# A block of gated values in its natural row order in DRAM, picked apart by the loads instead of by the store

## The chip, the cores and the metric

The kernel runs on one core of one Trainium2 chip. The metric is the device time of one execution in microseconds (us), lower is better. It is a single launch, and the numbers of this document are medians of several executions, or are read from one execution that the hardware profiler recorded.

## What is computed

The input is 8 sequences of 1024 tokens with 512 float32 channels. Two layers with residuals follow each other. The first is an adapter picked by the sequence's language (512 to 128 to 512), with a layer norm. The second is a recurrent cell, and the change lies in it. Cut to what matters:

```python
x = x + layernorm(x + relu(x @ W1 + b1) @ W2 + b2) * gamma0 + beta0      # per language
ctx    = causal_ema(x, tau_ctx)                     # h[t] = alpha * h[t-1] + x[t]
wg     = sigmoid(concat(x, ctx) @ Wg.T + bg)
gated  = x * wg                                     # "g" in the kernel
mod    = 0.5 + sigmoid(gelu(x @ Wn1.T + bn1) @ Wn2.T + bn2)      # 8 values per token
traces = [causal_ema(gated * mod[:, d], tau[d]) for d in range(8)]
temporal = sum_d traces[d] * softmax(blend)[d]
gate = sigmoid(temporal @ Wtemp.T + btemp)
soma = gelu(x @ Wsoma.T + bsoma)
x = x + layernorm((soma * gate) @ Wout.T) * gamma1 + beta1
```

## The kernel before

The 8192 tokens are worked off in 16 tiles (k = 0 to 15) of 512 tokens, two to a sequence. A tile has NB = 4 blocks of P = 128 tokens, and a block has NI = 4 spans of L = 32 tokens. `slot(k)` is written once for each engine; in slot k an engine does the end of tile k-1, the recurrence of tile k and the first layer of tile k+1, in a fixed order written out by hand. There is no planner: each engine runs its own list in order, and semaphores join the lists.

Large products run as three passes over a value split into a high and a low part (`split_product`, all its matmuls are recorded at L861). PE is TensorE, DVE VectorE, ACT ScalarE, POOL GpSimd. SP (SyncE) issues every DMA and computes nothing; all DMAs share its one queue.

The recurrence of a tile goes so:

- `value_gate(b)` (PE, L861) makes the gate's logits of block b, `gate_logits(b)` (DVE, L768) adds the bias, `open_gate(b)` (ACT, L490) takes the sigmoid, and `gated(b)` (DVE, L772) multiplies with x. The result is `g[:, b, :]` in SBUF, one token per partition, 512 floats (2 KB) each. It is signalled by `g_ready`.
- The recurrence inside the spans needs another arrangement, `grep` (4 spans by 512 channels in each partition): partition q*32 + s holds, for q = 0 to 3, the tokens s, 32+s, 64+s and 96+s of the block. [...] There are two buffers, `grep[b % 2]`.
- `products(b, hh, c)` (DVE, L763, four per block) multiplies `grep` with weights into `U`. `within_spans(b, hh)` (PE, L1005) takes U against the decay tables `Arep`.
- `span_states()` (PE at L987, DVE at L778) gives the states of the spans, V, and needs all four blocks of g. `from_before(b)` (PE, L1014) adds what comes from earlier spans. `trace(b)` (ACT, L494), `trace_by_channels(b)` (PE, L1026), `trace_high(b)` (ACT, L439) and `trace_low(b)` (DVE, L651) turn the result for the next product.

SP's list around the change, for one tile, is: `store_spans(0)`, `repeat_spans(0)`, `store_spans(1)`, `store_spans(2)`, `repeat_spans(1)`, `store_spans(3)`, `repeat_spans(2)`, `repeat_spans(3)`, then the store of x1 of the next tile (`keep_x1`, L277), and in the next slot the loads of x (L269) and of its transpose (L272). In this list `store_spans(b)` waits for `g_ready` of block b. `repeat_spans(b)` waits until the store of block b has landed (`g_stored[b]`, L320), and for b = 2 and 3 also until the products of block b-2 have been made (L322), since the buffer is theirs. For b = 1 there is no second wait.

DVE's list around it is: `gate_logits(2)`, `gated(2)`, products (0,0,0) and (0,0,1), `gate_logits(3)`, product (0,1,0), `gated(3)`, products (0,1,1) and (1,0,0), `span_states`, the last three products of block 1, the first two of block 2, `trace_low(0)`, the other two of block 2, the first two of block 3, `trace_low(1)`, and the last two. PE's is `value_gate(3)`, `soma_of(1)`, `within_spans(0, ...)`, `span_states`, `soma_begun(2)`, `from_before(0)`, `within_spans(1, 0)`, `soma_ended(2)` and so on. So PE can't pass the wait for V at `from_before(0)`, and V stands in DVE's list behind the first product of block 1.

Of the kernel before, what the change touches and what calls it, by code (L numbers as in the profile page):

```python
# [4 lines left out]
P = 128  # L5
BATCHES, SEQ, C = 8, 1024, 512
# [5 lines left out]
NB = TOK // P  # L12
NC = C // P
L = 32
NI = P // L
# [25 lines left out]
def cond_resid_kernel(nc, x, xc, ids, w1, w2, b1, b2, g0, be0, wg, wn1, wsoma, wtemp, wout, wn2,  # L41
                      bg, g1, be1, cols, taus, bn2, blend, eye, bits, out):
    F = mybir.dt.float32
# [8 lines left out]
    with ctx:  # L52
        def sb(name, shape, dt=F):
            return ctx.enter_context(nc.sbuf_tensor(name, shape, dt))

        def sb_two_ways(name, shape):

            with nc.sbuf_tensor(f"{name}_f", shape, F) as plain:
                pass
            return plain, sb(f"{name}_r", shape, R)  # L60
# [4 lines left out]
        def sem(name):  # L65
            return ctx.enter_context(nc.semaphore(name))
# [37 lines left out]
        grep = [sb(f"grep_{n}", [P, NI, C]) for n in range(2)]  # L104
# [11 lines left out]
        g, soma_hi = sb_two_ways("g", [P, NB, C])  # L116
# [9 lines left out]
        mv0, mv1 = (V[0][:, at:at + 2 * NB].rearrange("p (b s) -> p b s", s=2) for at in (192, 208))  # L126
        rows4 = sb("rows4", [P, 4, NB])
        rstd0, rstd1, minus_half, ema_last = (rows4[:, n, :] for n in range(4))
        g_dram = nc.dram_tensor("g_spans", [NB, L, NI * C], F, kind="Internal").ap()
        x1_dram = nc.dram_tensor("x1_tiles", [2, P, NB * C], F, kind="Internal").ap()  # L130


# [31 lines left out]
        g_stored = [sem(f"g_stored{n}") for n in range(NB)]  # L164
        grep_in = [sem(f"grep_in{n}") for n in range(2)]
# [32 lines left out]
        def upto(per_tile, tile, j):  # L198

            return tile * per_tile + (j + 1)  # L200

        def parts_of(k):

            return 0 < k <= TILES, 0 <= k < TILES, 0 <= k + 1 < TILES
# [49 lines left out]
        @block.sync  # L254
        def _(sp):
            def load_language(batch):

                one = sp.value_load(lang[0:1, batch:batch + 1], min_val=0, max_val=LANGS - 1)
                sp.dma_start(W1[:, :, :], w1[bass.ds(one, 1)].rearrange("a (n p) m -> p (a n) m", p=P)).then_inc(ld_lang, 16)
                sp.dma_start(W2_raw[:, :], w2[bass.ds(one, 1)].rearrange("a p m -> p (a m)")).then_inc(ld_lang, 16)  # L260
                sp.dma_start(b1_col, b1[bass.ds(one, 1)].rearrange("a (p m) -> p (a m)", p=P)).then_inc(ld_lang, 16)
                for row, src in ((b2_row, b2), (gamma0_row, g0), (beta0_row, be0)):
                    sp.dma_start(row[:, :], src[bass.ds(one, 1)].to_broadcast([P, C])).then_inc(ld_lang, 16)

            def load_split(n, src):
                sp.dma_start(halves[n][2], src.rearrange("(n p) m -> p n m", p=P)).then_inc(ld_split[n], 16)

            def load_x(tile):
                sp.dma_start(x_t[:, :, :], x[tile].rearrange("(n p) c -> p n c", p=P)).then_inc(ld_x, 16)  # L269

            def load_xT(tile):
                sp.dma_start(xT[:, :, :], xc[tile].rearrange("(n p) t -> p n t", p=P)).then_inc(ld_xT, 16)  # L272

            def keep_x1(tile):

                sp.wait_ge(x1_ready, upto(4, tile, NB - 1))
                sp.dma_start(x1_dram[tile & 1], x1[tile & 1][:, :, :].rearrange("p b c -> p (b c)")).then_inc(x1_stored, 16)  # L277

            def first_loads():

                sp.dma_start(lang[:, :], ids).then_inc(ld_ids, 16)
                sp.dma_start(alpha[:, 0, :], taus).then_inc(ld_small, 16)
                sp.dma_start(blend_c, blend).then_inc(ld_small, 16)
                sp.dma_start(con, bits).then_inc(ld_small, 16)
                sp.dma_start(ident[:, :], eye).then_inc(ld_small, 16)
                sp.dma_start(col, cols).then_inc(ld_small, 16)
                sp.dma_start(bn2_row[:, :], bn2.to_broadcast([P, D])).then_inc(ld_small, 16)
                load_xT(0)
                sp.wait_ge(ld_ids, 16)
                load_language(0)  # L290
                load_x(0)
                load_split(0, wn1)
                load_split(1, wsoma)
                load_split(2, wg[0:C])
                sp.dma_start(Wn2[:, :], wn2).then_inc(ld_rows, 16)
                for row, src in ((bg_row, bg), (gamma1_row, g1), (beta1_row, be1)):
                    sp.dma_start(row[:, :], src.to_broadcast([P, C])).then_inc(ld_rows, 16)

            def second_loads():

                sp.wait_ge(full["h"], upto(1, 0, 0))
                load_xT(1)
                load_split(3, wg[C:2 * C])
                sp.wait_ge(x1_ready, upto(4, 0, NB - 1))
                load_x(1)
                load_split(4, wtemp)
                load_split(5, wout)
                keep_x1(0)

            def slot(k):  # L310
                has_prev, has_cur, has_next = parts_of(k)

                def store_spans(b):
                    sp.wait_ge(g_ready, upto(4, k, b))
                    sp.dma_start(g_dram[b].rearrange("s (i c) -> i s c", i=NI), g[:, b, :]).then_inc(g_stored[b], 16)

                def repeat_spans(b):


                    sp.wait_ge(g_stored[b], 16 * upto(1, k, 0))  # L320
                    if b >= 2:
                        sp.wait_ge(U_ready, upto(PIECES, k, 4 * (b - 2) + 3))  # L322
                    elif b == 0 and has_next:
                        sp.wait_ge(x1_ready, upto(4, k + 1, NB - 1))
                    for q in range(NQ):
                        sp.dma_start(grep[b % 2][q * L:(q + 1) * L, :, :].rearrange("p i c -> p (i c)"),  # L326
                                     g_dram[b]).then_inc(grep_in[b % 2], 16)

                if has_prev:
                    if has_next:  # L330
                        if k & 1:
                            load_language((k + 1) // 2)
                        sp.wait_ge(U_ready, upto(PIECES, k - 1, 3 * PIECES // 4 - 1))
                        load_x(k + 1)
                        sp.wait_ge(U_ready, upto(PIECES, k - 1, PIECES - 1))
                        load_xT(k + 1)
                        sp.wait_ge(full["h"], upto(1, k + 1, 0))
                    else:
                        sp.wait_ge(U_ready, upto(PIECES, k - 1, PIECES - 1))
                    sp.dma_start(x1_back[:, :, :].rearrange("p b c -> p (b c)"), x1_dram[(k - 1) & 1]).then_inc(ld_back, 16)  # L340
                    for b in range(NB):
                        sp.wait_ge(res_ready, upto(4, k - 1, b))
                        sp.dma_start(out_tiles[k - 1, b * P:(b + 1) * P, :], res[:, b, :]).then_inc(stored, 16)
                else:
                    second_loads()
                if has_cur:
                    store_spans(0)
                    repeat_spans(0)
                    store_spans(1)
                    store_spans(2)  # L350
                    repeat_spans(1)
                    store_spans(3)
                    repeat_spans(2)
                    repeat_spans(3)
                if has_next:
                    sp.wait_ge(x1_stored, 16 * upto(1, k, 0))
                    keep_x1(k + 1)

            first_loads()
            for k in range(TILES + 1):  # L360
                slot(k)
            sp.wait_ge(stored, 16 * NB * TILES)
            sp.wait_ge(x1_stored, 16 * TILES)
# [795 lines left out]
```

## Time and profile before

| | us |
|---|---|
| median of 3 runs | 1514.78 |
| lowest, highest | 1514.3, 1514.91 |
| the profiled execution | 1509.55 |
| its span, first to last instruction | 1507.8 |
| PE busy in the span | 1372.3 (91%) |
| DVE busy | 1019.1 (68%) |
| ACT busy | 515.4 (34%) |
| POOL busy | 393.2 (26%) |
| mean granted clock of PE | 0.975 |
| mean DMA rate | 124 GB/s |

How to read it: busy times are sums over the whole span, and "busy" for PE counts modelled ends of pipelined matmuls, so 91% is not PE at its peak. The page's other parts used below are the chain of work that ended last (the last instruction followed back through what released it), the list of DMA issues with the median time from issue to landing, the waits by who waited for whom, timelines of one engine in order of time, and tables by stretch ("windows") with the busy time of each engine, the granted clock of PE as a fraction of full speed, the share of time in which the 16 DMA engines were busy, and what they moved.

### The profile page before, as it was taken

To read this page: it belongs to the slowest core of one execution; us is meant where nothing else is said; L and a number is where in the kernel's file an instruction comes from. 1 tells how busy PE (TensorE), PEld (TensorE's weight loads), DVE (VectorE), ACT (ScalarE), POOL (GpSimd) and SP (SyncE) were. 2 spreads that over 40 slices of the span, in tenths; PEclk is the share of its full clock that TensorE was granted. 3 is DMA by queue.
4 is the path that set the end of the run, shared out by engine and by line. 5 is a ranking of instruction groups with operands and counts; after the bars stand their busy time and mean duration, and the time that the engine had idled before them with its cause. 6 is when DMAs were issued, how large, how long until landed. Compare 5 with 4: busy or idle time off the path is not lost.

```text
span 1507.8 us, 19538 instructions
## 1 busy us (share of the span) xinstructions
PE 1372.3 (91%) x7836; PEld 977.2 (65%) x7836; DVE 1019.1 (68%) x1493; ACT 515.4 (34%) x812; POOL 393.2 (26%) x295
## 2 busy tenths in 40 slices
PE   2689989999999999999998998999999999998985
PEld 1566858576685766757576685757758576685744
DVE  6868676685667857577684767668576685767363
ACT  2324333242333424333242423424233332433323
POOL 4314123041330504123041422304133050411103
PEclk8799999999999999999999999999999999999999
DMA  7354351825427063361715526172541806334150
GB/s 240 112 144 143 95 161 60 203 77 138 141 61 226 35 165 109 107 194 49 201 44 144 170 71 181 57 193 93 134 146 58 228 29 168 113 99 125 49 144 32
DMA packets 66140, 186.22 MB, mean 124 GB/s; under 512 B 9090, under 2 KB 13826, under 8 KB 53762
## 3 DMA queue, kind: packets, MB, share of 16 engines
q1 hardware_dynamic: 66050, 184.97, 42.3%
q8 instruction: 62, 1.02, 0.3%
q14 instruction: 28, 0.23, 0.0%
HBM read 134.61 MB, written 50.33 MB: 123 GB/s over the span
## 4 chain that ended last, share of the span: by engine, by line
DVE 24%; DMA 21%; PE 19%; issue 13%; ACT 12%; SPq 3%; POOL 3%; POOLq 0%; DVEq 0%
DMA g_spans<-g_f 12%; PE ring L861 10%; DMA grep<-g_spans 9%; DVE U L763 7%; PE Tp L1014 4%; PE Tp L1005 4%; SPq L326 3%; ACT U L482 2%; DVE x L701 2%; DVE V L706 2%; DVE U L645 2%; DVE seq_lo L651 2%; DVE soma_r L659 2%; PE ring L854 2%; ACT g_r L448 2%
## 5 line engine op out<-in xcount | busy, mean ns | idle before, releaser
L763 DVE TENSOR_TENSOR U<-grep,w_qs 128x1024 f32<-128x1024 f32 x256 | 301.9, 1219 | 102.8 <-DMA grep<-g_spans 102.6
L385 POOL TENSOR_TENSOR x<-grep,b_row 128x512 f32<-128x512 f32 x64 | 81.9, 1312 | 668.1 <-DMA grep<-in_x 668.1
L1005 PE MATMUL Tp<-U,Arep 128*32 128x256 f32 x2048 | 153.0, 404 | 14.8 <-DVE U L763 13.8
L768 DVE TENSOR_TENSOR g_f<-ring,bg_row 128x512 f32<-128x512 f32 x64 | 44.2, 690 | 156.7 <-PE ring L861 156.6
L394 POOL TENSOR_TENSOR grep<-grep,beta_row 128x512 f32<-128x512 f32 x64 | 93.6, 1494 | 179.9 <-DMA grep<-x_tiles 179.9
L490 ACT ACTIVATE g_f<-g_f 128x512 f32<-128x512 f32 x64 | 40.5, 632 | 254.9 <-DVE g_f L768 254.7
L494 ACT ACTIVATE T_sb_f<-Tp 128x512 f32<-128x512 f32 x64 | 38.2, 598 | 260.7 <-PE Tp L1014 260.7
L1005 PEld LDWEIGHTS Tp<-U,Arep 128*32 128x32 f32 x2048 | 54.0, 112 | 105.0 <-DVE U L763 47.9
L861 PE MATMUL ring<-Wout_hi,g_r 128*128 128x512 f32 x256 | 102.2, 399 | 19.5 <-DVE soma_r L659 19.5
L861 PE MATMUL ring<-seq_hi,Wtemp_hi 128*128 128x512 f32 x256 | 106.8, 417 | 8.5 <-DVE seq_lo L651 8.5
L1014 PE MATMUL Tp<-V,Epow 128*128 128x512 f32 x128 | 76.7, 683 | 41.0 <-DVE V L778 41.0
L861 PE MATMUL ring<-x1T_hi,Wsoma_hi 128*128 128x512 f32 x256 | 109.8, 429 | 0.0
L861 PE MATMUL ring<-Wg_hi,seq_hi 128*128 128x512 f32 x256 | 100.4, 392 | 7.4 <-DVE Wg_r L562 7.4
L861 PE MATMUL ring<-Wg_hi,x1T_hi 128*128 128x512 f32 x256 | 103.1, 403 | 0.0
L861 PE MATMUL ring<-x1T_lo,Wsoma_hi 128*128 128x512 f32 x256 | 102.1, 399 | 0.0
L861 PE MATMUL ring<-x1T_hi,Wsoma_r 128*128 128x512 f32 x256 | 101.4, 396 | 0.0
L861 PE MATMUL ring<-Wout_r,g_r 128*128 128x512 f32 x256 | 100.4, 392 | 0.0
L861 PE MATMUL ring<-Wg_r,seq_hi 128*128 128x512 f32 x256 | 100.3, 392 | 0.0
L861 PE MATMUL ring<-Wout_hi,soma_r 128*128 128x512 f32 x256 | 100.2, 392 | 0.0
L861 PE MATMUL ring<-Wg_hi,seq_lo 128*128 128x512 f32 x256 | 100.1, 391 | 0.0
L861 PE MATMUL ring<-seq_hi,Wtemp_r 128*128 128x512 f32 x256 | 100.0, 391 | 0.0
L861 PE MATMUL ring<-Wg_hi,x1T_lo 128*128 128x512 f32 x256 | 100.0, 390 | 0.0
(151 smaller groups left out, 2865.5 us busy)
## 6 DMA issues: line engine op xcount, KB each, us to landing
grep<-g_spans SPq DMA_DIRECT2D x256, 256.0 KB, 5.0
grep<-in_xc SPq DMA_DIRECT2D x16, 1024.0 KB, 7.2
grep<-in_x SPq DMA_DIRECT2D x16, 1024.0 KB, 9.0
x_tiles<-x SPq DMA_DIRECT2D x16, 1024.0 KB, 7.6
g_spans<-g_f SPq DMA_DIRECT2D x64, 256.0 KB
grep<-x_tiles SPq DMA_DIRECT2D x16, 1024.0 KB, 4.8
out<-U SPq DMA_DIRECT2D x64, 256.0 KB, 2.0
gamma_row<-in_g SPq DMA_DIRECT2D x9, 256.0 KB, 7.3
```

Of the source, the lines that this page charges most:

```text
L326: sp.dma_start(grep[b % 2][q * L:(q + 1) * L, :, :].rearrange("p i c -> p (i c)"), g_dram[b]).then_inc(grep_in[b % 2], 16)
L385: nc.gpsimd.tensor_tensor(new[:, b, :], x_t[:, b, :], b2_row[:, :], ALU.add).then_inc(xb2_ready, 1)
L394: nc.gpsimd.tensor_tensor(x1_back[:, b, :], x1_back[:, b, :], beta1_row[:, :], ALU.add).then_inc(x1b_ready, 1)
L448: nc.scalar.activation(soma_hi[:, e, :], soma[:, e, :], ACT.Identity).then_inc(somahi_ready, 1)
L482: nc.scalar.activation(res[:, b, :], res[:, b, :], ACT.Identity, scale=rstd1[:, b:b + 1]).then_inc(scaled_ready, 1)
L490: nc.scalar.activation(g[:, b, :], g[:, b, :], ACT.Sigmoid).then_inc(sig_ready, 1)
L494: nc.scalar.activation(T_sb[b % 2][:, :], Tp[b % 2][:, :], ACT.Identity).then_inc(T_ready, 1)
L763: V_.tensor_tensor(U[:, (n + 2) % 4, :, :], grep[b % 2][:, :, at], w_qs[:, hh, at].unsqueeze(1).to_broadcast([P, NI, HC]), ALU.mult).then_ ...
L768: V_.tensor_tensor(g[:, b, :], bank_of("wg", k, b)[:, :], bg_row[:, :], ALU.add).then_inc(pre_ready, 1)
L861: last = nc.tensor.matmul(dst, lhsT(a, n), rhs(b, n), start=(first and n == begin and m == 0), stop=(final and n == steps - 1 and m == 2))
L1005: last = nc.tensor.matmul(Tp[b % 2][i * L:(i + 1) * L, at], Arep[:, b * NI + i, hh, :], U[:, (n + 2) % 4, i, :], start=(hh == 0 and c == 0 ...
L1014: nc.tensor.matmul(Tp[b % 2][:, :], Epow[:, odd * NB + b, :], V[odd][:, :], start=False, stop=True).then_inc(full["T"], 1)
```

## The change

The tensor in DRAM changes its shape from 32 rows of 8 KB per block (a row is one s with its four spans side by side) to the block's own 128 rows of 2 KB. Before, the store took the rows of 2 KB to their places in rows of 8 KB, through a destination that is walked as span, s, channel (sizes 4, 32, 512). Now the store writes the block as it stands in SBUF, 128 rows to 128 rows. The loads in turn read for each partition four pieces of 2 KB that lie 64 KB apart, where they read one row of 8 KB. The bytes in `grep`, the number of DMAs, their sizes, all waits and the order of every list are as before.

```diff
-        g_dram = nc.dram_tensor("g_spans", [NB, L, NI * C], F, kind="Internal").ap()
+        g_dram = nc.dram_tensor("g_blocks", [NB, P, C], F, kind="Internal").ap()
@@ store_spans(b)
                     sp.wait_ge(g_ready, upto(4, k, b))
-                    sp.dma_start(g_dram[b].rearrange("s (i c) -> i s c", i=NI), g[:, b, :]).then_inc(g_stored[b], 16)
+                    sp.dma_start(g_dram[b], g[:, b, :]).then_inc(g_stored[b], 16)
@@ repeat_spans(b)
                     for q in range(NQ):
-                        sp.dma_start(grep[b % 2][q * L:(q + 1) * L, :, :].rearrange("p i c -> p (i c)"),
-                                     g_dram[b]).then_inc(grep_in[b % 2], 16)
+                        sp.dma_start(grep[b % 2][q * L:(q + 1) * L, :, :],
+                                     g_dram[b].rearrange("(i s) c -> s i c", i=NI)).then_inc(grep_in[b % 2], 16)
```

## Rows read from the trace of the kernel before

**Rows 1.** The page's chain of work that ended last, by line, shares of span.
```profile
DMA g_spans<-g_f 12%; PE ring L861 10%; DMA grep<-g_spans 9%; DVE U L763 7%; PE Tp L1014 4%; PE Tp L1005 4%; SPq L326 3%; ACT U L482 2%; DVE x L701 2%; DVE V L706 2%; DVE U L645 2%; DVE seq_lo L651 2%; DVE soma_r L659 2%; PE ring L854 2%; ACT g_r L448 2%
```

**Rows 2.** Waits: who waited for whom, us in total, times, longest.
```profile
DVE U L763 <- DMA grep<-g_spans: 102.6, 50, 5.3
...
PE Tp L1014 <- DVE V L778: 41.0, 16, 3.9
```

**Rows 3.** Timeline of SP's issues in tile 7: start, us, line, what.
```profile
710.28 0.59 SPq L315 DMA_DIRECT2D g_spans<-g_f  x1
716.16 1.73 SPq L326 DMA_DIRECT2D grep<-g_spans  x4
717.93 4.45 SPq L315 DMA_DIRECT2D g_spans<-g_f  x2
725.09 1.70 SPq L326 DMA_DIRECT2D grep<-g_spans  x4
727.66 0.51 SPq L315 DMA_DIRECT2D g_spans<-g_f  x1
728.84 10.96 SPq L326 DMA_DIRECT2D grep<-g_spans  x8
```

**Rows 4.** Timeline of DVE in tile 7; in brackets idle before and releaser.
```profile
715.12 0.69 DVE L772 TENSOR_TENSOR g_f<-g_f,x 128x512 f32<-128x512 f32 x1 [0.60 <-ACT g_f L490]
...
721.16 0.69 DVE L772 TENSOR_TENSOR g_f<-g_f,x 128x512 f32<-128x512 f32 x1 [0.70 <-ACT g_f L490]
722.94 2.36 DVE L763 TENSOR_TENSOR U<-grep,w_qs 128x1024 f32<-128x1024 f32 x2 [1.09 <-DMA grep<-g_spans]
725.21 0.68 DVE L768 TENSOR_TENSOR g_f<-ring,bg_row 128x512 f32<-128x512 f32 x1
...
732.30 1.22 DVE L763 TENSOR_TENSOR U<-grep,w_qs 128x1024 f32<-128x1024 f32 x1 [3.54 <-DMA grep<-g_spans]
...
739.05 2.36 DVE L763 TENSOR_TENSOR U<-grep,w_qs 128x1024 f32<-128x1024 f32 x2 [1.52 <-DMA grep<-g_spans]
...
745.38 2.36 DVE L763 TENSOR_TENSOR U<-grep,w_qs 128x1024 f32<-128x1024 f32 x2 [1.10 <-DMA grep<-g_spans]
```

**Rows 5.** Timeline of PE in tile 7, behind its wait for V.
```profile
734.19 1.12 PE L1014 MATMUL Tp<-V,Epow 128*128 128x512 f32 x2 [1.99 <-DVE V L778]
```

**Rows 6.** Page's DMA issues: count, KB each, median us to landing.
```profile
grep<-g_spans SPq DMA_DIRECT2D x256, 256.0 KB, 5.0
...
grep<-in_x SPq DMA_DIRECT2D x16, 1024.0 KB, 9.0
...
grep<-x_tiles SPq DMA_DIRECT2D x16, 1024.0 KB, 4.8
out<-U SPq DMA_DIRECT2D x64, 256.0 KB, 2.0
```

**Rows 7.** Windows: stretch, us, busy by engine, granted clock, DMA share, GB/s.
```profile
712.00:716.00 4.00, 4.00 (x49) 3.09 (x48) 1.67 (x4) 0.63 (x1) 0.00 (x0) 1.00 0.22 63
...
727.00:734.00 7.00, 5.20 (x50) 2.63 (x49) 3.46 (x5) 1.55 (x2) 0.00 (x0) 1.00 1.02 247
...
753.00:755.00 2.00, 2.00 (x19) 1.73 (x16) 1.49 (x3) 2.00 (x5) 2.00 (x2) 1.00 1.02 397
```

**Rows 8.** Timelines of DVE and SP in tile 8, the latest of the tiles.
```profile
809.32 0.69 DVE L772 TENSOR_TENSOR g_f<-g_f,x 128x512 f32<-128x512 f32 x1 [0.70 <-ACT g_f L490]
...
813.73 1.70 SPq L326 DMA_DIRECT2D grep<-g_spans  x4
```

**Rows 9.** Windows: the 4 us behind the wait for V in tile 6.
```profile
643.50:647.50 4.00, 3.43 (x18) 1.10 (x18) 3.92 (x4) 0.60 (x1) 0.00 (x0) 0.57 0.54 129
```

**Rows 10.** Windows from store 0 of a tile to the next's: tiles 1, 2, 6.
```profile
170.05:258.16 88.11, 83.76 (x490) 59.94 (x489) 60.36 (x90) 30.84 (x49) 23.67 (x18) 1.00 0.42 120
258.16:350.31 92.15, 87.11 (x492) 61.57 (x491) 63.55 (x91) 31.81 (x51) 23.98 (x18) 0.96 0.46 129
...
619.87:710.28 90.41, 85.72 (x492) 60.77 (x491) 63.34 (x91) 31.93 (x51) 23.98 (x18) 0.98 0.46 132
```

## The prediction, made blind

> **What bounds the kernel now.** I read the chain of work that ended last first, to see which transfers stand on the path. The store of the gated block holds 12% of the span, the load that reads it back 9%, and issuing those loads 3% [rows 1]. The list of waits gives the same from the consumer's side: DVE stood 102.6 us before its products for the loads, and PE stood 41.0 us in 16 waits, one per tile, for V [rows 2]. PE is busy 91% of the span. So most of a tile is bound by PE, and one stretch by the way of the block through DRAM.
>
> The timelines show that stretch, here in tile 7. SP issues store 0 at 710.28 and the first load of block 0 at 716.16, which it may do once the store has landed: 5.88 us for 256 KB [rows 3]. Block 1 is what counts. Its values are ready at 715.81 (715.12 + 0.69) [rows 4], SP still waits for store 0, then issues four loads, and gets to store 1 at 717.93. Store 1 lands at about 725.05, and the load of block 1 starts at 725.09 [rows 3]. DVE gets it at 732.30, after 3.54 us of idling [rows 4]; PE, which needs V, made just behind that first product, has been idle for 1.99 us at 734.19 [rows 5]. The load of block 2 arrives at 739.05 and that of block 3 at 745.38; DVE waits for both, 1.52 and 1.10 us [rows 4]. So from 725 to 745 three loads follow each other, and the tile ends some 5 us behind the last.
>
> **The store: what it costs now and then.** A store of the same size and the same pieces, 128 rows of 2 KB, is in the kernel already: the output, with a destination that is just 128 rows. It lands 2.0 us after issue (median of 64), where the gated block's takes 5.88 [rows 3, 6]. In the window in which only that store moves, the 16 DMA engines are busy 0.22 of the time, which is three and a half engines, at 63 GB/s [rows 7]. A destination walked with 4 as its outermost size has evidently been dealt to few engines. After the change the outermost size is 128, as for the output, and I take 2.0 us.
>
> The Trainium skill has the rule for it (DMA: Bandwidth & Descriptors, section "Why a DMA increments its semaphore by 16 and not by 1"): a DMA runs on the largest number of engines up to 16 that divides the slowest dimension of both sides. That gives 4 before and 16 after, and the share of 0.22 agrees; by it the sum is the same as mine.
>
> **Where the gain goes, block by block**, in tile 7.
>
> Block 0: the store lands at 712.3, the loads are issued by 714.1 and land 5.0 us after issue [rows 6], about 719. Before they were awaited until 722.94. But in DVE's list the products stand behind `gated(2)`, which ends at 721.85, and behind two products comes `gate_logits(3)` at 725.21, which needs PE's `value_gate(3)` [rows 4]. So 1.09 us of waiting for the load turns into about 1 us of waiting for PE, and block 0 gives nothing.
>
> Block 1: store 1 is issued at 715.85, when it is ready, behind the loads of block 0 in the same queue, and lands with them or about 1 us behind, by 720.5. SP next has store 2 in its list, which waits for `gated(2)`: 721.87. It takes 0.51 us to issue, so the loads of block 1 start at 722.4 in place of 725.09: 2.7 us earlier. Here the wait for the store is replaced by the wait for the third block. In tile 8 the same two rows give 809.32 + 0.69 + 0.55 = 810.6 against 813.73, 3.1 us [rows 8]; the other tiles I read lie between 2.5 and 3.1. From first issue to DVE the load took 7.21 us, and a store spread over all engines now runs half a us ahead of it: 256 KB at the 247 GB/s of a full stretch [rows 7] is 1.1 us, of which at most half falls behind the load's own issue. I take 7.3: arrival at 729.7, against 732.30, so 2.6 us.
>
> PE then isn't kept: V would be ready at 729.7 + 1.2 + 0.6 = 731.5, and PE's work before it ended near 732.2 (734.19 less 1.99) [rows 5]. All of that idling goes.
>
> Block 2: its loads are issued at 728.84 as before, since product (0,1,1) hangs on PE and `gated(3)`. They landed 10.2 us later, because block 1 was on the wire. The gap between arrivals was 6.75 us for 1 MB, which at 247 GB/s needs 4.25; between them lay store 3, with all its bytes on a few engines. It now costs every engine the same 1.1 us. So the arrival lies between 729.7 + 5.4 = 735.1 and 729.7 + 6.75 = 736.4, against 739.05: 2.6 to 3.9 us.
>
> Block 3: issued when block 1's products are made, before at 737.6 (inside the row of 728.84, the last 8 us after its start), now at 729.7 + 1.2 + 0.6 + 3.5 = 735.0. It took 7.75 us, now 6.7 (four issues of 0.43 and 5.0) to 7.75: 741.7 to 742.8 against 745.38, so 2.6 to 3.6 us. Behind it the same products, two `trace_low` and PE's last pieces follow in 5 to 6 us. PE had about 14.4 us of work between 735.2 and 751.2, and starts on it at 733, so it permits up to 3.6 us. I take 2.6 us per tile, and 16 times that is 42 us.
>
> **The clock.** Behind the wait for V, PE's granted clock fell to half (1.2 GHz) in most tiles: over the four us behind it, tile 6 shows 0.57 [rows 9], and of sixteen such windows eleven lie between 0.50 and 0.73, five at 1.00. PE had been idle just before, 2.6 us in the mean and 3.9 at most [rows 2]. With that idling gone I expect no fall there. What a fall costs is bounded by whole tiles: tiles 2 and 6, with the same work, took 92.15 and 90.41 us, the first with a mean clock of 0.96, the second with 0.98 [rows 10]. So between 0 and 1.7 us each; most even tiles are like the cheap one, in which later waits hid the slow stretch. I take 0.9 for eleven tiles, 10 us.
>
> **The loads.** Their rows of 8 KB become four pieces of 2 KB. Nothing in the trace shows just that. From below: with every row 8 KB the loads keep the engines at a share of 1.02 and move 247 GB/s; in a window in which the transposed x is loaded, in pieces of 2 KB that also lie apart, the same share moves 397 GB/s [rows 7]. So a piece of 2 KB costs an engine 0.08 us, and 32 of them 2.6 us, under the 4.25 that a load has in any case; something other than the size of the pieces sets 247, and the price is nothing, or a little below. From above: 1 MB of x in pieces of 2 KB takes 9.0 us to land, 1 MB of x1 in rows of 8 KB 4.8 [rows 6]; all of that difference, 4.2 us, is the dearest it can be. But x is issued behind the last load and the 1 MB store of x1 in the same queue, which explains the 9.0 without the pieces. I take 0, being nearest to the window of 397. SP's issue of a load stays near 0.43 us; if 128 pieces cost it what they cost store 3, 0.51 us [rows 3], a block's four issues would take 0.3 us more, which is inside the range.
>
> The Trainium skill would explain the 247 (SBUF — State Buffer, section "Door 1: The DMA port swizzle"): 32 or 64 neighbouring partitions reach only 8 of 16 ports. By it the pieces are free. Against the change stands its rule of a fixed overhead of about 3 cycles per packet (DMA: Bandwidth & Descriptors, "Why small descriptors are slow (HBM only)"): 4 x 67 cycles for 259, 3.5% of 4.25 us, 0.15 us a load; by that the sum would be some 5 us smaller. No run here shows it.
>
> **The sum.** 42 + 10 = 52 us off the profiled execution's 1509.55 is 1457.5. The median lies 5.2 above that execution, so 1514.78 - 52 = 1463. Nothing else changes: between the tile's end and the next store 0 each engine's list starts from that end, x is loaded earlier by the same amount, and output stores are untouched.
>
> **Rivals.**
>
> Only part is passed on (15%). Store 1 lands late behind the loads, or PE, ACT and the trace steps behind block 3 take half back, as they may with 1.5 us less of slack. 1 to 1.6 us per tile and 5 us of clock: 21 to 31 us, 1484 to 1494. Against it: 1.3 us of room between store 1's landing and its use, and 3.6 us of room on PE.
>
> The loads eat the store's gain (8%): slower than before. Three loads in a row lie on the path, the first and third in full, since block 2's is overlapped. With a price d per load the arrival of block 3 is 742.3 + 2d against 745.38, so it decides from d = 1.5 us, a third of the data's time. With d halfway to the bound, 2.1, it is 1.1 us per tile, 18 us: 1533; at 4.2 about 5.5 us, 1603. For it speaks only the row of 9.0 us.
>
> The change doesn't do what it says (4%): the store isn't spread and keeps its 5.9 us. Then nothing moves, and it is 1512 to 1517. Against it stands the output's row of the same form.
>
> **Chances and range.** The forecast has 73%, its own range 2.0 to 3.4 us per tile and 3 to 14 us of clock: 35 to 68 us, 1447 to 1480. With most of the first rival the range is 1446 to 1490. By 0.2%, about what a measurement of this kernel can tell from no change: faster 0.88, the same 0.05, slower 0.07.
>
> **What would show it.** After the change, the time from store 0's issue to SP's first load issue should be near 2.1 us. The loads of block 1 should start 0.55 us behind the end of `gated(2)`. DVE's waits for the loads should fall from 102.6 to some 30 us, and PE's for V from 41.0 to under 5, with the clock at 1.00 behind it; DVE's wait for PE at L768 should grow by about 16 us. The load's median of 5.0 us tells d: over 6.5 the slower rival holds. If the loads arrive earlier as said and the tile doesn't, the steps behind block 3 are what I misjudged.

## The result, and the profile after

The changed kernel takes 1455.46 us (median of 4, 1450.32 to 1457.57) against 1514.54 us for the kernel before on the same chip: a ratio of 0.9608, 95% interval 0.9581 to 0.9636. That is 59 us less, where 52 were forecast (1463 us, range 1447 to 1480). The profiled execution has a span of 1454.6 us, 53.2 less than before.

The chain that ended last, by engine and by line, on the page of the changed kernel:

```profile
PE 64%; DVE 20%; ACT 5%; issue 3%; DMA 2%; POOL 1%; SPq 0%; POOLq 0%; DVEq 0%
PE ring L861 51%; DVE U L763 6%; PE Tp L1005 5%; DVE soma_r L659 4%; PE Tp L1014 4%; DVE U L645 3%; DVE seq_lo L651 2%; DMA grep<-g_blocks 2%; ACT g_r L448 2%; DVE soma_f L656 2%; DVE x1T_lo L633 2%; PE ring L854 2%; ACT T_sb_f L494 2%; PE smp L968 1%; PE smp L987 1%
```

The store of the block, 12% of the chain in [rows 1], is gone from it, and the load has gone from 9% to 2%. PE's own work, the product helper at L861 above all, now leads to the end. The waits (us in total, times, longest) and the DMA issues (median us to landing last) say the same:

```profile
DVE g_f L768 <- PE ring L861: 179.7, 62, 6.4
...
DVE U L763 <- DMA grep<-g_blocks: 16.5, 29, 1.3
```

```profile
grep<-g_blocks SPq DMA_DIRECT2D x256, 256.0 KB, 4.4
...
g_blocks<-g_f SPq DMA_DIRECT2D x64, 256.0 KB, 2.0
```

DVE waits 16.5 us for the loads in place of 102.6, and PE's wait for V, 41.0 us in [rows 2], is no longer in the list. What grew is DVE's wait for PE at L768. The store lands in 2.0 us, as the output's does in [rows 6]; the load lands in 4.4 where it took 5.0.

Tile 11 is typical of the changed kernel. SP's issues (start, us, what), which answer to [rows 3]; L315 stores a block of gated values to DRAM, L326 reads it back in four loads of 32 partitions each:

```profile
1032.74 0.33 SPq L315 DMA_DIRECT2D g_blocks<-g_f  x1
1034.77 1.75 SPq L326 DMA_DIRECT2D grep<-g_blocks  x4
1038.30 6.38 SPq L315 DMA_DIRECT2D g_blocks<-g_f  x2
1044.72 1.87 SPq L326 DMA_DIRECT2D grep<-g_blocks  x4
1050.12 0.34 SPq L315 DMA_DIRECT2D g_blocks<-g_f  x1
1051.30 7.73 SPq L326 DMA_DIRECT2D grep<-g_blocks  x8
```

And DVE in the same tile, answering to [rows 4]:

```profile
1043.62 0.69 DVE L772 TENSOR_TENSOR g_f<-g_f,x 128x512 f32<-128x512 f32 x1 [0.70 <-ACT g_f L490]
1044.23 2.35 DVE L763 TENSOR_TENSOR U<-grep,w_qs 128x1024 f32<-128x1024 f32 x2
1047.67 0.69 DVE L768 TENSOR_TENSOR g_f<-ring,bg_row 128x512 f32<-128x512 f32 x1 [1.09 <-PE ring L861]
...
1051.49 1.23 DVE L763 TENSOR_TENSOR U<-grep,w_qs 128x1024 f32<-128x1024 f32 x1 [0.26 <-DMA grep<-g_blocks]
1053.14 0.69 DVE L778 TENSOR_TENSOR V<-smp,w_jd 120x512 f32<-120x512 f32 x1 [0.42 <-PE smp L987]
...
1057.83 2.36 DVE L763 TENSOR_TENSOR U<-grep,w_qs 128x1024 f32<-128x1024 f32 x2 [0.60 <-DMA grep<-g_blocks]
...
1067.79 2.35 DVE L763 TENSOR_TENSOR U<-grep,w_qs 128x1024 f32<-128x1024 f32 x2
```

Store 0 has landed at 1034.77, 2.03 us behind its issue (5.88 before). The loads of block 1 are issued at 1044.72, 11.98 us behind store 0, 0.41 us behind the end of `gated(2)` (1043.62 + 0.69); in tile 7 of before it was 14.81. DVE gets block 1 at 18.75 us behind store 0, in tile 7 of before at 22.02. Tile 7 itself went from 22.02 to 19.60, its third block of values being ready 0.8 us later than before; the mean over tiles 1 to 13 went from 22.5 to 19.1. V no longer waits for the load but for PE (0.42 us). The last product ends at 1070.14, 37.40 us behind store 0.

I call that time, from store 0's issue to the end of the last product, the stage, and what is left up to the next store 0 the tail. Read off the timelines in the same way for the 14 tiles 0 to 13:

| us | before | after |
|---|---|---|
| 14 tiles, store 0 to store 0 | 1260.8 | 1213.0 |
| of it stages | 582.1 | 527.1 |
| of it tails | 678.7 | 685.9 |
| one stage, tiles 1, 5, 7, 9, 13 of before (clock stays up) | 40.1 to 40.3 | |
| one stage, tiles 2 to 4, 6, 8, 10 to 12 (clock falls) | 41.3 to 43.4 | |
| stage of tile 0 | 43.8 | 38.2 |
| one stage after, tiles 2 to 4, 6, 8 to 13 | | 37.4 to 37.5 |
| one stage after, tiles 1, 5, 7 | | 38.2 |

The stages give 54.9 us. The tails, in which no instruction was changed, take 7.2 back.

### The profile page after: what moved, and what is told of

It reads as the page before. It is cut to its first block, busy times and chain, and to the rows that moved or that the text cites. A ratio compares the mean times of both kernels' runs of the same rounds, so it can differ in the third digit from the quotient of the medians.

```text
span 1454.6 us, 19538 instructions
## 1 busy us (share of the span) xinstructions
PE 1354.1 (93%) x7836; PEld 976.0 (67%) x7836; DVE 1030.6 (71%) x1493; ACT 515.0 (35%) x812; POOL 393.0 (27%) x295
## 4 chain that ended last, share of the span: by engine, by line
PE 64%; DVE 20%; ACT 5%; issue 3%; DMA 2%; POOL 1%; SPq 0%; POOLq 0%; DVEq 0%
PE ring L861 51%; DVE U L763 6%; PE Tp L1005 5%; DVE soma_r L659 4%; PE Tp L1014 4%; DVE U L645 3%; DVE seq_lo L651 2%; DMA grep<-g_blocks 2%; ACT g_r L448 2%; DVE soma_f L656 2%; DVE x1T_lo L633 2%; PE ring L854 2%; ACT T_sb_f L494 2%; PE smp L968 1%; PE smp L987 1%
## 5 line engine op out<-in xcount | busy, mean ns | idle before, releaser
L763 DVE TENSOR_TENSOR U<-grep,w_qs 128x1024 f32<-128x1024 f32 x256 | 301.7, 1219 | 18.1 <-DMA grep<-g_blocks 16.5
L768 DVE TENSOR_TENSOR g_f<-ring,bg_row 128x512 f32<-128x512 f32 x64 | 44.3, 692 | 179.7 <-PE ring L861 179.7
L1005 PE MATMUL Tp<-U,Arep 128*32 128x256 f32 x2048 | 144.0, 386 | 14.1 <-DVE U L763 13.5
L490 ACT ACTIVATE g_f<-g_f 128x512 f32<-128x512 f32 x64 | 40.5, 632 | 260.2 <-DVE g_f L768 260.1
L861 PE MATMUL ring<-Wout_hi,g_r 128*128 128x512 f32 x256 | 104.3, 407 | 25.2 <-DVE soma_r L659 25.2
L861 PE MATMUL ring<-seq_hi,Wtemp_hi 128*128 128x512 f32 x256 | 107.6, 420 | 8.5 <-DVE seq_lo L651 8.5
L494 ACT ACTIVATE T_sb_f<-Tp 128x512 f32<-128x512 f32 x64 | 38.2, 598 | 209.4 <-PE Tp L1014 209.4
L861 PE MATMUL ring<-Wg_hi,seq_hi 128*128 128x512 f32 x256 | 100.7, 393 | 8.8 <-DVE Wg_r L562 8.8
L861 PE MATMUL ring<-x1T_hi,Wsoma_hi 128*128 128x512 f32 x256 | 106.8, 417 | 0.0
L659 DVE TENSOR_TENSOR soma_r<-soma_f,g_r 128x512 fp32r<-128x512 f32 x64 | 73.8, 1153 | 44.7 <-ACT g_r L448 44.7
L861 PE MATMUL ring<-Wg_hi,x1T_hi 128*128 128x512 f32 x256 | 103.2, 403 | 0.0
L861 PE MATMUL ring<-Wout_hi,soma_r 128*128 128x512 f32 x256 | 101.9, 398 | 0.0
L861 PE MATMUL ring<-Wout_r,g_r 128*128 128x512 f32 x256 | 101.8, 397 | 0.0
L861 PE MATMUL ring<-seq_hi,Wtemp_r 128*128 128x512 f32 x256 | 100.6, 393 | 0.0
L861 PE MATMUL ring<-Wg_r,seq_hi 128*128 128x512 f32 x256 | 100.5, 393 | 0.0
L861 PE MATMUL ring<-Wg_hi,seq_lo 128*128 128x512 f32 x256 | 100.5, 393 | 0.0
L861 PE MATMUL ring<-x1T_hi,Wsoma_r 128*128 128x512 f32 x256 | 100.4, 392 | 0.0
L861 PE MATMUL ring<-seq_lo,Wtemp_hi 128*128 128x512 f32 x256 | 100.4, 392 | 0.0
L861 PE MATMUL ring<-Wg_hi,x1T_lo 128*128 128x512 f32 x256 | 99.9, 390 | 0.0
```

The costliest lines, as they stand in the source:

```text
L490: nc.scalar.activation(g[:, b, :], g[:, b, :], ACT.Sigmoid).then_inc(sig_ready, 1)
L494: nc.scalar.activation(T_sb[b % 2][:, :], Tp[b % 2][:, :], ACT.Identity).then_inc(T_ready, 1)
L659: V_.tensor_tensor(soma_lo[:, e, :], soma[:, e, :], soma_hi[:, e, :].bitcast(F), ALU.subtract).then_inc(somalo_ready, 1)
L763: V_.tensor_tensor(U[:, (n + 2) % 4, :, :], grep[b % 2][:, :, at], w_qs[:, hh, at].unsqueeze(1).to_broadcast([P, NI, HC]), ALU.mult).then_ ...
L768: V_.tensor_tensor(g[:, b, :], bank_of("wg", k, b)[:, :], bg_row[:, :], ALU.add).then_inc(pre_ready, 1)
L861: last = nc.tensor.matmul(dst, lhsT(a, n), rhs(b, n), start=(first and n == begin and m == 0), stop=(final and n == steps - 1 and m == 2))
```

## The experiments

Each was run beside the kernel before on the same chip, on three chips in all, so ratios are compared rather than times. On these chips the kernel before had medians of 1509 to 1512 us, with single runs from 1500 to 1523, so a difference of less than some 5 us between two kernels isn't told apart. The changed kernel was run on one of them, the chip of `load1_sooner`, `other_ports` and `filled_wait`:

> The changed kernel itself, on the same chip and beside the same runs of the kernel before as the three others of this call, as their measure. Both theories: 1450 to 1460 us, a ratio near 0.961.

It took 1456.4 us, a ratio of 0.9656 (0.9596 to 0.9716). The loads landed in 4.4 us again.

**Is it the store or the loads?** In `split_store` the DRAM layout and the 8 KB loads stay as before, and a block is stored in four parts, all of which the loads await:

```diff
-        sp.dma_start(g_dram[b].rearrange("s (i c) -> i s c", i=NI), g[:, b, :]).then_inc(g_stored[b], 16)
+        for i in range(NI):
+            sp.dma_start(g_dram[b][:, i * C:(i + 1) * C], g[i * L:(i + 1) * L, b, :]).then_inc(g_stored[b], 16)
```

> The layout and the 8 KB loads of the kernel before; each block is stored by four DMAs of 32 partitions, one for each span, so that each store's outermost size is 32 in place of 4. Theory 1 (the gain is the store's spread over all engines): store 0 has landed about 3.3 us after its first issue (four issues of 0.43 and 2.0) in place of 5.9; the four issues of store 2 delay the loads of block 1 by 1.3 us against the changed kernel, so about 1465 to 1480 us. Theory 2 (the gain is mostly in the loads, whose pieces are smaller and which landed in 4.4 in place of 5.0 us): the loads keep 5.0 us, and the time stays above 1495 us.

1467.9 us (ratio 0.9743, 0.9692 to 0.9794): inside theory 1. In DRAM the bytes lie 2 KB wide and 8 KB apart as in the kernel before, and yet a part lands 2.0 us after issue. The parts are also smaller, 64 KB, so this run alone leaves open whether it is the outermost size that counts; `few_engines` below keeps 256 KB, and together they say that the outermost size made the store slow and not the strided destination. The 12 us to the changed kernel go to SP. In tile 11 it needs 1.72 us for the issues of store 0, where one issue takes 0.33, and its loads may start 3.03 us behind the first of them. The loads of block 1, behind the four issues of store 2, start 1.78 us behind the end of `gated(2)` in place of 0.41, and over the 14 tiles the stages sum to 538.3 us in place of 527.1:

```profile
1042.59 1.72 SPq L316 DMA_DIRECT2D g_spans<-g_f  x4
1045.62 1.70 SPq L327 DMA_DIRECT2D grep<-g_spans  x4
```

`few_engines` is the changed kernel with its store put back on few engines; its loads step over the unused row of the padded tensor, with pieces of 2 KB as before:

```diff
-        g_dram = nc.dram_tensor("g_blocks", [NB, P, C], F, kind="Internal").ap()
+        g_dram = nc.dram_tensor("g_blocks", [NB, NI, L + 1, C], F, kind="Internal").ap()
-        sp.dma_start(g_dram[b], g[:, b, :])
+        sp.dma_start(g_dram[b, :, 0:L, :], g[:, b, :])
```

> The changed kernel with one unused row of 2 KB behind every 32 rows in DRAM, so that the store's destination is again walked as 4, 32, 512; the loads read 2 KB pieces 66 KB apart. Theory 1: store 0 takes 5.9 us again, DVE's waits for the loads return, PE's clock falls again behind the wait for V, and the time is 1500 to 1515 us. Theory 2: the loads stay at 4.4 us and most of the gain stays, under 1480 us.

1511.8 us, a ratio to the kernel before of 1.0019 (0.9987 to 1.0052): the whole gain is gone, with the loads still in pieces of 2 KB. In the window of tile 11 in which only the store moves the engines are busy 0.21 of the time, where [rows 7] have 0.22; the changed kernel moves the same 256 KB within two microseconds. The first row is `few_engines`, the second the changed kernel (stretch, us, busy by engine, clock, DMA share, GB/s):

```profile
1073.00:1076.00 3.00, 3.00 (x44) 2.27 (x43) 1.13 (x3) 0.63 (x1) 0.00 (x0) 1.00 0.21 74
```

```profile
1033.00:1035.00 2.00, 2.00 (x10) 1.65 (x10) 0.13 (x1) 0.00 (x0) 0.00 (x0) 1.00 0.36 136
```

DVE's waits and the loads' median are those of the kernel before, and PE's clock falls again behind the wait for V in 10 of the 14 tiles:

```profile
DVE U L763 <- DMA grep<-g_blocks: 99.1, 51, 5.4
```

```profile
grep<-g_blocks SPq DMA_DIRECT2D x256, 256.0 KB, 5.0
```

**What does the size of a piece cost?** `wide_pieces` reads four neighbouring rows at once, `pieces_1k` the two halves of a row apart; the stores are those of the changed kernel:

```diff
-        sp.dma_start(grep[b % 2][q * L:(q + 1) * L, :, :],
-                     g_dram[b].rearrange("(i s) c -> s i c", i=NI))
+        sp.dma_start(grep[b % 2][q * L:(q + 1) * L, :, :].rearrange("p i c -> p (i c)"),
+                     g_dram[b].rearrange("(s i) c -> s (i c)", i=NI))
```

and in `pieces_1k` instead

```diff
+        sp.dma_start(grep[b % 2][q * L:(q + 1) * L, :, :].rearrange("p i c -> p (i c)").rearrange("p (h i c) -> p h i c", h=2, i=NI),
+                     g_dram[b].rearrange("(i s) (h c) -> s h i c", i=NI, h=2))
```

> The changed kernel, whose loads read four neighbouring rows (8 KB in one piece) for each partition; the block's tokens then stand at other places than the computation wants, so the output differs, with the same instructions, bytes and waits. It isolates the size of the pieces. If the pieces of 2 KB are what made the loads faster (4.4 us), they are back at 5.0 us and the time is 5 to 15 us above the changed kernel, 1460 to 1470. If the loads are faster because no store lingers on a few engines, they stay at 4.4 us, and the time at 1455 us within 4. If pieces of 2 KB cost something, they land below 4.4 us and the time is lower.

> The changed kernel, whose loads take pieces of 1 KB (the two halves of a row apart; channels then stand at other places, so the output differs). If each piece has a price, the loads' median rises from 4.4 us by as much again as 2 KB against 8 KB cost; with 0.08 us per 2 KB piece in the x loads an engine-bound load would need up to 64 x 0.08 = 5.1 us of data time in place of 4.25, so 5.2 us and about 1470. If ports or something else than pieces set the rate, 4.4 us and 1455 us within 4.

With pieces of 8 KB the loads land in 4.5 us and the time is 1460.2 us (ratio 0.9690, 0.9640 to 0.9740). With pieces of 1 KB they land in 4.5 us too, and it is 1465.7 us (0.9727, 0.9676 to 0.9778). So from 1 to 8 KB the landing depends on the piece by 0.1 us at most. Both times are above the 1455 within 4 that I had written beside an unchanged landing. DVE's waits for the loads are 24.8 us with pieces of 8 KB and 36.8 with 1 KB, against 16.5 and 17.6 in the two runs of the changed kernel, so 2 KB is the best of the three, if by little. With pieces of 1 KB part of it is SP's time: the four issues of the first block's loads in tile 7 take 2.58 us, where the changed kernel's take 1.75. That this makes the whole 1465.7 us isn't shown: in the profiled execution the stages of 14 tiles are only 1.7 us longer than the changed kernel's, the tails 4.4. The first row is `pieces_1k`:

```profile
691.59 2.58 SPq L326 DMA_DIRECT2D grep<-g_blocks  x4
```

```profile
690.50 1.75 SPq L326 DMA_DIRECT2D grep<-g_blocks  x4
```

The loads became faster because of the stores: in all kernels whose stores are spread and whose loads keep their order, they land in 4.4 to 4.6 us, with 8 KB pieces (`split_store`, `wide_pieces`) as with smaller ones; with stores on few engines 5.0.

**Which store matters?** Three kernels put only some blocks through the padded tensor of `few_engines` (`apart` is the tuple of those blocks; their loads read from that tensor):

```diff
-        sp.dma_start(g_dram[b], g[:, b, :])
+        sp.dma_start(g_apart[b, :, 0:L, :] if b in apart else g_dram[b], g[:, b, :])
```

> The changed kernel, in which block 0 alone goes through a tensor with an unused row behind every 32, so that its store lies on few engines (5.9 us). Theory 1 (what counts is when the loads of block 1 may start, and that hangs on the third block): the loads of block 0 start 3.9 us later and still arrive about when the DVE asks for them, store 1 lands near 12.8 us behind store 0's issue in place of 12.0, so the loads of block 1 start 0.5 to 1 us later, and the time rises by 3 to 15 us, to 1459 to 1471. Theory 2 (each store gives its own 3.9 us): a quarter of the gain is lost, 1468 or more.

1460.9 us (0.9644, 0.9591 to 0.9698). It isn't apart from the changed kernel, and the interval leaves out the loss of a quarter of the gain (0.9706 from the result's ratio). Store 0's 3.9 us are mostly hidden, as forecast: over 14 tiles the stages are 4.4 us longer than the changed kernel's, 0.3 us per tile.

> The same for blocks 0 and 1: both stores on few engines. Theory 1: store 1 lands 14.8 us behind store 0's issue, as in the kernel before, the loads of block 1 start 2.6 us later than in the changed kernel, and more than half of the gain is lost: 1485 to 1500 us, and the clock falls again behind the wait for V in some tiles. Theory 2: half of the gain, 1482.

1481.0 us (0.9794, 0.9740 to 0.9847). Here nearly half of the gain is gone. That is the number that I had written beside the theory that each store gives its own share, which `slow_store_0` and the next run rule out, and less than I had expected of the other, 1485 or more. In tile 11 the loads of block 1 start 14.90 us behind store 0, as late as in the kernel before, and block 1 is there at 1069.21, after 7.08 us. But behind it block 2 catches up, arriving at 27.1 us behind store 0 where it came at 28.7 in tile 11 before, and the stage is 39.6 us, where it was 42.0 in that tile before and 40.1 to 40.3 in tiles whose clock stayed up. The clock, which I had expected to fall in some tiles, falls behind the wait for V in one.

```profile
1047.23 0.60 SPq L317 DMA_DIRECT2D g_apart<-g_f  x1
...
1062.13 2.72 SPq L328 DMA_DIRECT2D grep<-g_apart  x4
```

```profile
1069.21 1.23 DVE L766 TENSOR_TENSOR U<-grep,w_qs 128x1024 f32<-128x1024 f32 x1 [3.45 <-DMA grep<-g_apart]
```

> The same for blocks 2 and 3 alone. Nobody waits for their landing. If only landing times matter, nothing changes, 1456 within 4. If what counts is that a store on few engines stands in front of the next loads on those engines (64 KB on an engine, some 2.6 us, against 16 KB), the loads of blocks 1 and 2 arrive about 2 us later, their median goes from 4.4 to 5 us or more, and the time is 1475 to 1495 us.

1510.9 us, ratio 0.9988 (0.9955 to 1.0021): all of the gain is gone, from two stores whose landing holds up next to nothing (SP waits for that of store 2 by 0.3 to 0.5 us in tiles 1 to 15, and block 2 arrives within 0.6 us of when DVE asks for it). That is beyond the 1475 to 1495 that I had expected. In tile 11:

```profile
1072.39 0.33 SPq L317 DMA_DIRECT2D g_blocks<-g_f  x1
...
1083.98 0.59 SPq L317 DMA_DIRECT2D g_apart<-g_f  x1
1084.62 2.65 SPq L328 DMA_DIRECT2D grep<-g_blocks  x4
```

```profile
1095.00 1.23 DVE L766 TENSOR_TENSOR U<-grep,w_qs 128x1024 f32<-128x1024 f32 x1 [4.13 <-DMA grep<-g_blocks]
```

The loads of block 1 start 12.23 us behind store 0, as early as they can, 0.64 us behind store 2. But they arrive after 10.38 us, where the changed kernel's take 6.77 (1044.72 to 1051.49): 3.6 us more. My reading is that store 2 stands in front of them on the few engines that it uses, and that a load has landed only when its slowest engine is through. The views don't show single engines, but the length fits: at the 63 GB/s of [rows 7] the store's 256 KB take 4.2 us (an estimate), less the 0.64 us of its head start 3.5. The 2.6 us that I had written before the run was too small, because it took the rate of a stretch with all engines at work. Even SP's issues are held up, 2.65 us for four in place of 1.87. Block 1 is used at 22.6 us behind store 0, in tile 7 of the kernel before at 22.0. So a store on few engines costs this kernel one of two things: landing late itself, which starts the loads 2.7 us late, or standing in front of them. Either alone brings block 1 back to 22 us or more in tile 11, and both together, in the kernel before, cost no more than the second alone. The first alone costs less in the whole: with slow stores 0 and 1 PE waits 20.7 us for V in all, with slow stores 2 and 3 it waits 42.6, and its clock falls behind that wait in 8 of the 14 tiles.

**What does the clock cost?** `filled_wait` is the kernel before with six matmuls made twice on PE, in front of `from_before(0)`:

```diff
+                    if again:
+                        split_product(ps[:, :], lambda a, n: Wsoma[a][:, n, at], lambda a, n: x1T[a][:, n, :], NC // 2)
...
-                    soma_begun(2)
+                    soma_begun(2, again=True)
                     from_before(0)
```

> The kernel before with six more matmuls (1.35 us at full clock, a product that is made twice) on PE in front of from_before(0), so that PE idles 1.3 us less in its wait for V while everything else stays. It prices the fall of PE's clock by itself. If a fall costs 0.9 us in eleven tiles, as predicted, and the filling prevents most of them, the time falls by 5 to 12 us against the kernel before, and the granted clock behind the wait is 1.00 in most tiles. If the falls cost nothing because later waits hide them, it stays within 3 us. If the matmuls stand on the path, it rises, by up to 20 us.

It took 1507.7 us, ratio 0.9978 (0.9947 to 1.0010), 3 us less by the medians and anything from 8 less to 2 more by the interval, where 5 to 12 had been expected. The clock behind the wait is up: tile 10 of the kernel before (first row) and of `filled_wait` (second row), each over 4 us.

```profile
1001.80:1005.80 4.00, 3.45 (x18) 1.10 (x18) 3.90 (x4) 0.60 (x1) 0.00 (x0) 0.57 0.60 156
```

```profile
1003.20:1007.20 4.00, 3.45 (x24) 1.76 (x24) 3.90 (x4) 0.60 (x1) 0.00 (x0) 1.00 0.55 131
```

PE idled 0.66 us there, and the fall is gone, as in all tiles but the first. But the run is no clean price of a fall. Its stages over the 14 tiles sum to 570.9 us, 11.2 less than in the kernel before, and its tails to 689.2, 10.5 more. Two falls came to the tails instead, in tiles 2 and 4, each of them 51.5 us long in place of 49.0. And in the profiled execution the granted clock was 0.95 over more than half of the span, which I can't explain and which its own time (1508.24 us, in the middle of the ten) doesn't show:

```profile
520.00:850.00 330.00, 317.72 (x1878) 226.55 (x1877) 225.67 (x321) 114.88 (x181) 80.94 (x62) 0.95 0.45 133
860.00:1390.00 530.00, 507.14 (x2956) 364.59 (x2955) 374.21 (x534) 185.02 (x295) 137.64 (x104) 1.00 0.42 121
```

A cleaner price lies in the trace of `slow_store_23`, where block 1 arrives 22.6 to 22.7 us behind store 0 in every tile from 1 to 14 but tile 5, and the clock falls in some of them and not in others. Here are tiles 11 and 12, first PE's row behind the wait for V (start, us, idle before), then the window of the whole stage:

```profile
1096.88 1.12 PE L1017 MATMUL Tp<-V,Epow 128*128 128x512 f32 x2 [2.58 <-DVE V L781]
1185.03 2.08 PE L1017 MATMUL Tp<-V,Epow 128*128 128x512 f32 x2 [2.68 <-DVE V L781]
1072.39:1112.63 40.24, 36.52 (x273) 23.40 (x272) 26.05 (x29) 8.02 (x12) 0.00 (x0) 1.00 0.67 182
1160.44:1202.21 41.77, 38.58 (x276) 24.12 (x274) 25.97 (x29) 8.42 (x13) 0.00 (x0) 0.96 0.70 180
```

The wait is the same within 0.1 us and the tails are both 47.8 us, but the stage with the fall is 1.5 us longer. Of its tiles 1 to 14, six keep the clock up and take 40.2 to 40.5 us, seven with a fall take 41.6 to 41.9 (tile 5, whose block 1 came late, 42.7). So a fall costs the tile about 1.5 us where it occurs. What the whole run gains when the falls are prevented is another matter, since some come back in the tails.

**Two further steps.** `load1_sooner` moves `repeat_spans(1)` ahead of `store_spans(2)`; `other_ports` issues a block's loads in the order 0, 2, 1, 3; the last kernel does both.

> The changed kernel with the loads of block 1 issued ahead of store 2 in SP's list, so that they no longer wait for the third block. Theory 1 (the loads are all but hidden now, DVE waits for them 16.5 us in all and PE is the bound): the loads of block 1 start some 4 us earlier, DVE's waits for loads fall to about 8 us, and the time falls by 2 to 8 us against the changed kernel, since the waits for block 2 stay (its loads hang on the buffer). Theory 2 (the arrival of block 1 still sets the tile): at least 12 us less.

> The changed kernel with the four loads of a block issued for partitions 0 to 31, 64 to 95, 32 to 63, 96 to 127 instead of in rising order. If the rate of 210 to 250 GB/s comes from one 32-partition load alone reaching half of the ports, and neighbours in the queue overlap enough to use both halves, the loads' median falls from 4.4 to under 4.0 us and the time by up to 5 us. If the loads run strictly one after another, nothing changes: 4.4 us and within 3 us.

> The changed kernel with both small edits that seemed to help: the loads of block 1 ahead of store 2, and the loads in the order 0, 64, 32, 96. Each took a few of the 16.5 us that DVE waits for loads. If they add, DVE's waits fall to about 6 us and the time is 1450 to 1454. If PE is the bound by now, 1453 to 1457, as each alone.

They took 1453.5 us (0.9634, 0.9571 to 0.9697), 1454.2 (0.9620, 0.9562 to 0.9677) and 1451.7 (0.9605, 0.9562 to 0.9647). In DVE's list of waits the loads go from 17.6 us in the changed kernel's second run to 13.1 (8 expected), 10.1 and 6.6 (6 expected), so each does its part; the load's median falls to 4.2 and 4.1 us in the two with the other order (under 4.0 expected). In the time they are not told apart from the changed kernel: DVE's waits were all but hidden already. The row of `sooner_and_ports`:

```profile
DVE U L763 <- DMA grep<-g_blocks: 6.6, 18, 1.1
```

## Why the prediction was right, point by point

**The store's price** was right: 5.88 us before, 2.03 now, and 2.0 in the median of 64. That few engines were the cause, read from the share of 0.22 and the output's row, is shown by `split_store` and `few_engines` together: the strided destination remains in the one, the loads' pieces of 2 KB in the other, and the time goes with the outermost size of the store.

**Block 0** was right: DVE's 1.09 us of waiting for the load became 1.09 us of waiting for PE, and `slow_store_0` shows that store 0's landing hardly matters (0.3 us per tile).

**Block 1.** Its loads start 0.41 us behind `gated(2)` (0.55 forecast). Over tiles 1 to 13 they start 2.6 us earlier in the mean (2.7 forecast for tile 7) and reach DVE after 6.9 us in place of 7.7, so block 1 is at DVE 3.4 us earlier. In tile 7 itself, for which the sum was made, it is 2.4 us earlier, not 2.6: the third block of values was late there by 0.8 us, and the load took 6.8 us where 7.3 were forecast. The term that I mis-sized is what the stores do to the loads behind them. I took tile 7's 7.2 us, which is among the shortest of the tiles, as the load's own and added to it for store 2 running ahead; it contained some waiting for stores on few engines already. `slow_store_23` shows how much that can be, 3.6 us, when the store is just in front. But not all of the surplus was of use: PE's `span_states` became the next thing to be late (0.42 us in DVE's row for V), so less than all of it is passed on.

**Blocks 2 and 3.** The stage is 37.4 us, against 40.2 in tiles whose clock stayed up: 2.8 us, for the 2.6 of the sum. The steps behind block 3 took nothing back within the stage.

**The clock.** No tile's clock falls behind the wait for V any more, as forecast. Its size was too small, and its count was off: of the sixteen windows that I had read, ten lie below 1.00 and six at 1.00, not eleven and five. The stages of before with a fall were longer than 40.2 by 1.9 us in the mean of eight, 15.5 us in all. Part of that is late loads: the longest wait, in tile 8, was 5.24 us where tile 7's was 3.54. But at the same wait of PE the pair of tiles in `slow_store_23` differs by 1.5 us, so much of it is the clock: a fall costs about 1.5 us there, where the sum had 0.9. What the run as a whole gets of it is less, by what the tails give back: `filled_wait` shortens the stages by 11 us and the run by 3.

**What I had not seen** is that the tails would change. They take 7.2 us back. In tiles 0, 4 and 6 the clock now falls some 60 us behind store 0, where PE waits in the next slot, and their tails are 50.5 to 50.7 us in place of 48.9 to 49.1: 5 us. Here is such a place in tile 6 of the changed kernel:

```profile
660.00:664.00 4.00, 1.32 (x4) 0.99 (x4) 3.30 (x5) 2.81 (x6) 2.21 (x2) 0.82 0.01 2
```

PE is busy for 1.32 of these 4 us, with no DMA at work. The rest is that the tails of tiles 1 and 3 are 48.9 us where they were 47.8, a length that an odd tile has once in the kernel before too (tile 13). So the sum over 14 tiles is 39 us by the step of 2.8 us, 16 by the longer stages of eight tiles that are gone, and 7 given back: 48 (tile 0's longer stage before, and the 0.8 us more in four tiles after, cancel). The forecast's terms for 14 tiles are 36, 9 and nothing. Each term came out larger than forecast, by 3 and by 7 us, and the 7 us given back, which the forecast didn't have, cancel the second. That the total came out so close is partly luck.

**The rivals.** That only part is passed on was wrong in size: it had 1 to 1.6 us per tile, and the stage gave 2.8. That the loads would eat the gain was wrong, and more clearly than I had weighed it: the price d is not above 0.1 us from 8 down to 1 KB (4.5, 4.4 and 4.5 us). So the 9.0 us of x can't be laid to its pieces; that its place in the queue makes them was not tried.

**The rules of the Trainium skill that stand in the prediction.** Its fixed overhead per packet (DMA: Bandwidth & Descriptors, "Why small descriptors are slow (HBM only)") would have made 8 KB pieces the quicker by 0.15 us a load, an estimate from the page's cycles; the trace shows 4.5 us for them and 4.4 for 2 KB, so it isn't seen here. Its rule on the number of engines (Trainium skill, DMA: Bandwidth & Descriptors, "Why a DMA increments its semaphore by 16 and not by 1") agrees with every run: with 4 outermost on one side the engines' share was 0.21 or 0.22 and store 0 took 5.8 to 6.0 us, with 128 or 32 a store landed in 2.0. For its rule on ports (Trainium skill, SBUF — State Buffer, "Door 1: The DMA port swizzle") the landing of 4.2 against 4.4 us, with the loads' order changed, is a weak sign at most.

**The checks that I had named**: the first load issue 2.03 us behind store 0 (2.1); the waits for loads at 16.5 us (30) and for V at none (under 5); L768 up by 23 us (16); the loads' median 4.4 us, far from the 6.5 of the slower rival.

## What to carry to other kernels

Look at the outermost size on both sides of every DMA: a walk that begins with a 4 can put a quarter of a megabyte on few of the sixteen engines, and the share of DMA time in a window in which it moves alone tells it. Such a transfer costs twice, in its own landing and in every transfer queued behind it, so ask not only who waits for it but what stands behind it; two stores whose landing held up next to nothing cost this kernel its whole gain. Where a rearrangement can be done by the side that reads or by the side that writes, give it to the one whose outermost size stays large; pieces of 2 KB were as good as 8 KB.

## What the hardware showed that I had not expected

- In `slow_store_23` the loads of a block right behind a store on few engines took 10.4 us in place of 6.8, and SP took 2.65 us for its four issues in place of 1.87.
- Pieces of 1, 2 and 8 KB land in the same 4.4 to 4.5 us in loads to 32 partitions; pieces of 1 KB cost SP's issue, 2.58 us for four DMAs against 1.75.
- Where PE's idling ended in one place, its clock began to fall in another, 60 us behind store 0, in 3 of 14 tiles. A fall behind the wait for V cost about 1.5 us in the tiles of `slow_store_23`. Why the clock fell in these tiles and not in the others stays open, as does the step of 1.1 us in the tails of odd tiles.
